# Second attention: order of TensorE's work in a group, places of the turns in the ring, and two copies on ScalarE

## What is computed

```python
q = (x @ Wq).reshape(b, n, N_HEADS, HEAD_DIM)
k, v = jnp.split(ctx @ Wkv, 2, axis=-1)
q = apply_axial_rope(q, pos_map)
k = apply_axial_rope(k, ctx_pos_map)
scale = 1.0 / np.sqrt(HEAD_DIM).astype(np.float32)
logits = jnp.einsum('bqhd,bkhd->bhqk', q, k) * scale
w = jax.nn.softmax(logits, axis=-1)
attn = jnp.einsum('bhqk,bkhd->bqhd', w, v)
attn = attn.reshape(b, n, N_HEADS * HEAD_DIM)
return attn @ Wout + bout
```

## Time and profile before

| | us |
|---|---|
| median of 3 runs | 1728.85 |
| lowest and highest | 1728.18 and 1734.74 |
| the profiled execution, as timed | 1729.65 |
| its span, from the first to the last instruction | 1727.9 |
| of it the second attention's groups | 651.8 to 1026.3 |
| mean granted clock of TensorE | 0.965 of full speed |

### The profile page before, as it was taken

The page is one execution under the profiler, slowest core; times in us unless marked ns, Lnnn a source line. Parts: engine busy times, 40 slices in busy tenths (PEclk is TensorE's granted clock), DMA queues, the critical chain, the costliest instruction groups (busy, mean ns, idle before and its releaser), DMA issues. The chain is left out here.

```text
span 1727.9 us, 25136 instructions
## 1 busy us (share of the span) xinstructions
PE 1615.1 (93%) x8556; PEld 1188.6 (69%) x8556; DVE 1066.3 (62%) x1959; ACT 784.2 (45%) x1239; POOL 457.4 (26%) x422
## 2 busy tenths in 40 slices
PE   6987689999959889999999989989999999999998
PEld 5776679999947653433343347668888888888886
DVE  5886733222248877898888837655555547545456
ACT  5653223332334526878877763453333332223232
POOL 1210023332237751111110001332322223233232
PEclk8998789999988978999999999999999999999999
DMA  8996126663255764222232211443333246422221
GB/s 271 340 359 227 55 80 228 233 223 138 74 183 173 241 182 107 76 67 65 75 75 62 70 20 49 151 166 125 103 115 126 84 160 256 164 68 76 87 68 49
DMA packets 110364, 236.40 MB, mean 137 GB/s; under 512 B 39888, under 2 KB 53840, under 8 KB 101536
## 3 DMA queue, kind: packets, MB, share of 16 engines
q1 hardware_dynamic: 104000, 214.33, 37.1%
q0 software_dynamic: 6240, 20.45, 3.5%
HBM read 274.84 MB, written 93.45 MB: 213 GB/s over the span
## 5 line engine op out<-in xcount | busy, mean ns | idle before, releaser
L1319 DVE TENSOR_REDUCE early_top<-r_ring 128x1 f32<-128x512 f32 x480 | 304.2, 680 | 33.6 <-PE r_ring L1330 29.3
L2045 ACT ACTIVATE r_probs<-r_st 128x1024 f32<-128x1024 f32 x256 | 248.0, 1021 | 42.7 <-PE r_st L1958 39.9
L48 PE MATMUL f_bank<-late_xnT,late_weights 128*128 128x512 f32 x1056 | 252.4, 392 | 0.0
L48 PEld LDWEIGHTS f_bank<-late_xnT,late_weights 128*128 128x128 f32 x1056 | 196.8, 188 | 40.9 <-issue 0.7
L2835 DVE TENSOR_TENSOR attn<-attn,f_bank 128x512 f32<-128x512 f32 x132 | 90.7, 687 | 195.0 <-PE f_bank L48 130.7
L48 PE MATMUL m_bank<-w_place,m_xT 128*128 x936 | 168.1, 329 | 3.0 <-DVE m_xT L1220 3.0
L2829 ACT ACTIVATE attn<-f_bank 128x512 f32<-128x512 f32 x132 | 78.9, 598 | 180.0 <-PE f_bank L56 125.5
L48 PEld LDWEIGHTS m_bank<-w_place,m_xT 128*128 128x128 f32 x936 | 153.5, 191 | 6.9 <-issue 3.6
L1330 PE MATMUL r_ring<-early_slots 48*128 48x512 f32 x352 | 141.1, 475 | 4.9 <-PEq L1372 1.3
L1330 PEld LDWEIGHTS r_ring<-early_slots 48*128 48x128 f32 x352 | 58.6, 186 | 118.7 <-DVE early_top L1319 109.4
L1987 PE MATMUL r_out<-r_probs,early_v 128*17 128x512 f32 x1024 | 136.5, 605 | 0.5 <-ACT r_probs L2045 0.3
(11 more groups left out here) (330 smaller groups left out, 2788.5 us busy)
## 6 DMA issues: line engine op xcount, KB each, us to landing
w_place<-expert_split SPq DMA_DIRECT2D x72, 1408.0 KB
w_place<-expert_split SPq DMA_DIRECT2D x36, 1024.0 KB
late_w_dram<-late_weights SPq DMA_DIRECT2D x11, 1920.0 KB, 8.1
expert_split<-w_place SPq DMA_DIRECT2D x10, 1408.0 KB
w_place<-expert_split SPq DMA_DIRECT2D x36, 384.0 KB
late_weights<-late_w_dram SPq DMA_DIRECT2D x11, 1024.0 KB, 5.1
late_weights<-late_w_dram SPq DMA_DIRECT2D x11, 896.0 KB, 4.8
early_slots<-y_rows SPq DMA_DIRECT2D x16, 512.0 KB, 7.3
```

The lines of the kernel that those rows point to most:

```text
L48: last = nc.tensor.matmul(out, l, r, start=(i == 0), stop=(i == len(passes) - 1))
L1319: return nc.vector.reduce_max(self.top[g % 2][:, q, h:h + 1], bank[:], AXIS_X)
L2045: nc.scalar.activation(probs[k][:, 2 * pair:2 * pair + 2, :], st_ps[pair][:], ACT.Exp, scale=SCALE).then_inc(exp_done, 1)
```

## The change

The steps, their number and their sizes stay. Three things move.

- **Places.** `SHIFT_PLACE` becomes 2 and `OUT_PLACE` 10. The maxima now have places 0, 1, 3 to 5 and so on: 0, 1, 3, 4 for q = 0; 5 to 8 for q = 1; 9, 11, 12, 13 for q = 2; 14 to 17 for q = 3.
- **TensorE's order** of a step is written out in one piece instead of a loop over k. V(1), V(2) and V(3) now mostly stand between two pairs of maxima. T follows V(3) of the group before directly, and O stands between S(2,1) and a maximum. Before, T and O came after a V and one maximum.
- **ACT's order.** The copy of the shifts comes before the copy of the out rows, and the copy of the sums stands one exponential later, after E(2,0).

```diff
         PLACES = KT * GROUP + 2
-        SHIFT_PLACE, OUT_PLACE = GROUP, 2 * GROUP + 1
+        SHIFT_PLACE, OUT_PLACE = 2, 10
...
-            return q * GROUP + h + min(q, 2)
+            n = q * GROUP + h
+            return n + (n >= SHIFT_PLACE) + (n >= OUT_PLACE - 1)
...
             for g in range(GROUPS):
-                for k in range(KT):
-
-                    def maxima_of(*heads):
-                        if g + 2 < GROUPS:
-                            maxima(g + 2, k, heads)
-
-                    maxima_of(0)
-                    scores(g, k, 0)
-                    maxima_of(1)
-                    scores(g, k, 1)
-                    maxima_of(2)
-                    if k:
-                        values(g, k - 1)
-                    elif g:
-                        values(g - 1, KT - 1)
-                    maxima_of(3)
-                    if k == 0 and g + 1 < GROUPS:
-                        turn_shifts(g + 1)
-                    if k == 1 and g:
-                        turn_out(g - 1)
+                scores(g, 0, 0)
+                scores(g, 0, 1)
+                maxima_ahead(g, 0, 0, 1)
+                if g:
+                    values(g - 1, 3)
+                if g + 1 < GROUPS:
+                    turn_shifts(g + 1)
+                maxima_ahead(g, 0, 2)
+                scores(g, 1, 0)
+                maxima_ahead(g, 0, 3)
+                scores(g, 1, 1)
+                maxima_ahead(g, 1, 0, 1)
+                values(g, 0)
+                maxima_ahead(g, 1, 2, 3)
+                scores(g, 2, 0)
+                maxima_ahead(g, 2, 0)
+                scores(g, 2, 1)
+                if g:
+                    turn_out(g - 1)
+                maxima_ahead(g, 2, 1)
+                scores(g, 3, 0)
+                maxima_ahead(g, 2, 2, 3)
+                values(g, 1)
+                maxima_ahead(g, 3, 0)
+                scores(g, 3, 1)
+                maxima_ahead(g, 3, 1, 2)
+                values(g, 2)
+                maxima_ahead(g, 3, 3)
...
             for g in range(GROUPS):
...
+                exponentials(g, 0, 0)
+                exponentials(g, 0, 1)
+                if g + 1 < GROUPS:
+                    copy_shifts(g + 1)
+                if g:
+                    copy_out(g - 1)
+                exponentials(g, 1, 0)
+                exponentials(g, 1, 1)
+                exponentials(g, 2, 0)
+                if g:
+                    copy_sums(g - 1)
+                exponentials(g, 2, 1)
+                exponentials(g, 3, 0)
+                exponentials(g, 3, 1)
```

More of the change, by code:

```diff
@@ L1998, in turn_out, with maxima_ahead @@
                 last.then_inc(out_turned, 1)
+            def maxima_ahead(g, q, *heads):
+                if g + AHEAD < GROUPS:
+                    maxima(g + AHEAD, q, heads)
             for g in range(GROUPS):
-                for k in range(KT):
-                    def maxima_of(*heads):
-                        if g + 2 < GROUPS:
-                            maxima(g + 2, k, heads)
-                    maxima_of(0)
-                    scores(g, k, 0)
-                    maxima_of(1)
-                    scores(g, k, 1)
-                    maxima_of(2)
-                    if k:
-                        values(g, k - 1)
-                    elif g:
-                        values(g - 1, KT - 1)
-                    maxima_of(3)
-                    if k == 0 and g + 1 < GROUPS:
-                        turn_shifts(g + 1)
-                    if k == 1 and g:
-                        turn_out(g - 1)
+                scores(g, 0, 0)
[26 more added lines that the diff above has]
+                maxima_ahead(g, 3, 3)
             values(GROUPS - 1, KT - 1)
@@ L2039, in copy_sums, with exponentials @@
                                      ACT.Copy).then_inc(sums_copied, 1)
+            def exponentials(g, k, pair):
+                act.wait_ge(scores_ready, (g * KT + k) * 2 + pair + 1)
+                nc.scalar.activation(probs[k][:, 2 * pair:2 * pair + 2, :], st_ps[pair][:], ACT.Exp,
+                                     scale=SCALE).then_inc(exp_done, 1)
             for g in range(GROUPS):
[L2042 to L2053, removed]
+                exponentials(g, 0, 0)
[12 more added lines that the diff above has]
+                exponentials(g, 3, 1)
             copy_out(GROUPS - 1)
```

## The result

| | before | changed |
|---|---|---|
| median, us | 1730.05 (4 runs) | 1711.65 (4 runs, 1708.20 to 1717.37) |
| profiled execution, its span | 1727.9 | 1706.5 |
| second attention's groups in it | 651.8 to 1026.3 | 648.5 to 1007.1 |
| steady part, 29 steps | 338.43 | 323.39 |
| one step | 11.67 | 11.15 |

The ratio is 0.990 with a 95% interval of 0.9865 to 0.9935: about 1% faster. A later comparison of the same two kernels gave 0.993 (0.9907 to 0.9953). The forecast was 1708, in a range of 1697 to 1720.

What follows compares the result with a forecast made beforehand. TensorE and DVE were taken to limit each other through three banks, DVE needing 10.57 of 11.67 us. A 10.94 us step saves 0.73, 21.2 us over 29 steps: 1708.5 profiled, 1707.7 after the median offset, say 1708; range 1697 to 1720.

Steps and rivals of the forecast that it cites:

- What bounds the kernel: Steady stage: TensorE and DVE pass the limit through three banks; order loses 1.1 to 1.2 us of each 11.67 us step.
- The walk: Start-by-start timing of one changed step from V(2) to the next V(2), closing at 10.94 us instead of 11.67.
- m7: First maximum behind V(0): start after V(0) ends at 6.27, DVE's read at 6.66, with m8 and m9 at 7.28 and 7.90.
- m6's wait: Ahead of V(0): m6, due at 4.6, waits for m3's read and starts at 4.91, costing V(0) about 0.25 us.
- The sum: Whole step: 11.67 - 10.94 = 0.73 us saved, 21.2 us over 29 steps.
- The first and the last steps: Stage ends: first step at half clock, last two without maxima; given 0 gain, within 2 us.
- Edits priced at nothing: ACT's copies: out rows after shifts cost nothing, at most 0.60 uncovered; sums' copy costs nothing, with 0.1 us to spare.
- SyncE's queue: Shift rows for the next group arrive before S(0,0) needs them, with 1.6 us slack left, where 2.1 were.
- DVE as the bound: Rival: m6 and m12 lose nothing, step is DVE's 10.57 us, gain 32 us, total 1697; chance 0.10.
- Half the gain: Rival: sums' copy behind E(2,0) delays m13 and V(1); step 11.3, gain 10 us, total 1719; chance 0.14.
- The slower case: Rival: paired maxima do not run side by side; step 11.9 with m6's wait, 7 us slower, 1736; chance 0.06.
- The price from the Trainium skill: TensorE products: 215.7 ns start to start at 512 columns; would make the step 10.79 and gain 25 us; not used.

Runs made afterwards that it cites:

- the short reads: DVE reads 384 of each maximum's 512 columns, in both kernels: step 10.84 us against the changed kernel's 11.15, and 11.35 against 11.67 before.
- the run of four maxima put back: Changed kernel with m17 moved from behind V(2) to ahead of it, so m14 to m17 stand in one run: step 11.69 us against 11.15.
- The swap on ScalarE: Changed kernel with the out rows' copy put back ahead of the shifts' copy: step 11.15 us, unchanged; whole time 1708.10 us.
- one maximum moved across V(0): Changed kernel with m6 moved from ahead of V(0) to behind it: step 11.36 us against 11.15.
- one set alone ahead of T: Changed kernel with m(0,2) between V(3) and T, and the out rows copied first: step 11.05 us against 11.15; ratio to the kernel before 0.9903, later 0.9905.
- the kernel with the early copy of the sums: Changed kernel with ScalarE's copy of the sums put back ahead of E(2,0): mean step 13.60 us against 11.15; whole time 1780.94 us.
- the kernel with O behind V(0): Changed kernel with O at place 8, behind V(0) and one maximum, and the sums' copy ahead of E(2,0): step 11.72 us against 11.15.

## Why the prediction was right, and where it was not

**What bounds the kernel: half right.** Both engines wait on the ring of three banks, as the two waits in one stage said. But I read DVE as nearly the bound (10.57 of 11.67) and the lost time as DVE starving behind V and O. Most of the old order's loss is the round trip in its two runs with four maxima, 1.70 each where 1.13 would do: the short reads show it with DVE idle, and the run of four maxima put back shows it with full reads. I had named both waits, m2's and m16's, from the rows, and explained them by DVE having run behind. The rows had the answer already: DVE was idle 0.23 before the read at 803.48 that m16 waits for the earlier trace rows.

**The walk: right as a method.** It used each bank's release, and so held the round trip without my naming it. Its steps from V(2) to m7 are within 0.05 of the trace, and pairs run side by side (811.14, two maxima, 0.50 in all).

**The term that failed: m7.** I let DVE read m7 at 6.66, counted on from m3. But V(0) had just been moved to 5.28 by m6's wait, so that m7 could start at 6.27 and be read at 6.81, not 6.66. The trace has 6.85, and DVE idle 0.21 before it. From there the delay runs on. The reads of m8 and m9 in the changed kernel:

```profile
812.29 1.28 DVE L1319 TENSOR_REDUCE early_top<-r_ring 128x1 f32<-128x512 f32 x2
```

m9's read ends at 8.74 (813.57) instead of 8.58, and m12, which needs its bank, starts at 8.79 instead of 8.63. m13's read ends at 815.50 (811.68 + 3.82). m16, which needs that bank, starts at 815.56, V(2) 0.43 later, and the step closes at 11.16. O starts at 7.69 and not at 7.40, because it waits until m7 has been read. That is not what delays m12, since m12 waits for m9's read. It does delay m11, which can be read at 813.62 (813.08 + 0.54), a little after DVE is done with m9. DVE's later reads, m13's among them, come behind that.

The sum was 0.73 a step; it is 0.52. Times 29 that is 15.0 us instead of 21.2. The first and the last steps, which I priced at 0 within 2, gave 1.1.

**Edits priced at nothing.** The swap on ScalarE costs and brings nothing, as said. The sums' copy ended at 813.58 (813.18 + 0.40), 0.04 before m13 started at 813.62, where I had 0.1. So it cost nothing, but only just. In its old position the same copy costs 1.1 us a step at nearly the full clock, and more at the lower one. I had it as a rival's risk and not as what it is, the part of the edit that O's new place cannot do without.

**SyncE's queue.** The shift rows go out at 811.68, and their last bytes move before 815.0. S(0,0) starts at 816.97, with no wait for a transfer in the trace. The slack is 2.0 us, where I had 1.6. Half microseconds of the changed kernel (columns as in rows 1):

```profile
814.50:815.00 0.50, 0.50 (x8) 0.00 (x0) 0.50 (x2) 0.50 (x1) 0.00 (x0) 1.00 0.03 8
815.00:815.50 0.50, 0.50 (x8) 0.30 (x4) 0.50 (x2) 0.41 (x1) 0.00 (x0) 1.00 0.00 0
```

**The rivals.** DVE as the bound did not come: DVE is busy 303.51 of 323.39 us, 94% and not 97%. Half the gain did not come through ScalarE, though the true gain, 0.52, lies between this rival's 0.37 and the walk's 0.73. The slower case needed pairs that do not run side by side, and they do. The price from the Trainium skill, "TensorE: Matmul & The Clock Gate", section "Wait — 56ns, not 53.3ns?", 215.7 ns a product, would have given a step of 10.79, an estimate further off still. In the changed trace four turns, from 805.81 to 806.93, take 1.12, as before.

**The whole time** came out 3.7 us above the forecast, and that it came so close is partly luck. The profiled executions differ by 21.4 us, as much as I had forecast (21.2). But the steps gave only 15.0 of it, the first and last steps 1.1, and 5.3 came from outside the stage, where nothing was changed. The changed kernel's two medians, 1711.65 and 1718.97, lie 7.3 us apart. The test of the walk is the step, and there the gain was 0.52 and not 0.73.

## What to carry to other kernels

In a ring of n banks, count the results that a producer writes between two of its long steps. The (n+1)th cannot start before a whole round trip of the first (write, read, release), even when the reader is idle. Here that was 1.27 to 1.29 us with full reads, and it made a run of 1.13 last 1.70. So keep at most n of them in a run where it costs nothing else, and let the long step cover the round trip. Count again after each move: one maximum moved across V(0) took the wait along, and one set alone ahead of T cost 0.42 of the 0.53 that it saved. When an order is walked through, go over every step behind a delay again, the reader's start included: the error here was one read counted from before a wait that had just been added. When work is moved on one in-order engine, its counterpart on the other has to move too: the copy left in its old position made an order that gains 1% lose 3%.

## What the runs showed of the hardware

- The transposes of O start later behind a read's end than a product does. m7's read ends at 812.36 (811.68 + 0.68) and O starts at 812.52, 0.16 later. m12 at 813.62 starts 0.05 behind the end of m9's read (812.29 + 1.28), and m16 at 815.56 starts 0.06 behind m13's (815.50). O's wait stands in all 29 steps of the steady part, 5.1 us in sum. Why O starts later is not shown.
- Four more transposes of 8 columns, right behind four others, cost 0.43, not the 0.53 from T's start to the next product.
- In the kernel with the early copy of the sums TensorE waited for exponentials in every step, up to 1.0 us, and the granted clock went between 1.00 and 0.76 from one 20 us stretch to the next. At 0.76 the engine spends part of the stretch at 1.2 GHz instead of 2.4 GHz. In the kernel with O behind V(0), where such a wait is 0.64 to 0.7 in each step, the granted clock was 1.00 from 700 to 950. What makes the difference is not shown. Of the 2.45 us that the early copy of the sums costs a step, 1.10 are there at nearly the full clock (12.25 against 11.15), and the other 1.35 come with the lower one.
